# Remainders moved to VectorE, transposes of the probabilities and the projection moved within a pair, group means sooner

## The chip, the cores and the metric

The kernel runs on one core of one Trainium2 chip. The metric is the device time in microseconds (us) of one launch. Before the change it is 5577.6 us, the median of three runs (5576.49 to 5582.28).

## The reference

The input x is 8 images of 192 channels and 128x128 pixels. Two residual layers follow each other, each on a group norm of its input:

```python
# layer 1: attention in windows of 8x8 pixels, 6 heads of 32 channels
v, qk = x @ V_w.T + V_b, x @ QK_w.T + QK_b                # per pixel
o = irfft2(rfft2(q) * rfft2(k))                           # circular convolution in the window
attn = softmax(o @ v.T + bias)                            # 64x64 per head and window
y = attn @ v
x = x + (y @ proj_w.T + proj_b)
# layer 2: Laplacian and a 1x1 convolution
x = x + conv1x1(gn + laplacian(gn), merge_w) + merge_b    # gn = group_norm(x), 32 groups
```

The result has to be close to that of float32 throughout.

## The kernel before

**Units of work.** Two windows side by side are 128 pixels. The main loop works on doubles of such units: a *pair* in this text is one turn of `doubles()`, index j, 512 of them for the eight images, and four pairs make a *strip* of 8 image rows. The loop is a software pipeline written out by hand. In turn j the engines do step 0 of pair j (QKV, transposes of v), step 1 of pair j-1 (product in the frequency domain, inverse transform, scores), step 2 of pair j-2 (softmax), step 3 of pair j-3 (transposes of the probabilities, y) and step 4 of pair j-4 (projection). In the code `pair(k)` is true when there is a pair for step k.

**Engines.** Each engine runs its own list in the written order, and waits on semaphores (`wait_ge`). TensorE (PE) does the matmuls, ScalarE (ACT) copies from PSUM to SBUF and does the exponentials, VectorE (DVE) adds the position bias (L909, which writes `probs`), takes the maximum (L914), makes the remainders of q and k (L903), the frequency product (L920), the sum (L935), its reciprocal (L953), and the residual (L943). GpSimd (POOL) subtracts the maximum (L1225), multiplies by the reciprocal (L1246, semaphore `norm_done`), and computes the Laplacian of layer 2 (L1161, L1171, L1174) and the remainder of x (L1234). SyncE (SP) issues the DMAs.

**Two halves of a number.** float32 values are split into a rounded high part and a remainder, and matmuls of the parts are added. For the projection ACT writes the high parts `yh` and half of `yb` (`yh_out`), and POOL writes the remainders `yl` (L1251) and the other half of `yb` (L1253), each 256 columns, semaphore `yl_done`. `project()` (L582 to L587) does two matmuls on `yh`, then waits for `yl_done`, then does three more; it is called twice a pair, for channels 0 to 127 and 64 to 191.

**Banks.** `b_t` holds four PSUM banks. The frequency product L920 (`prod_done`) reads all four, and the transposes of the probabilities (L629) write two of them. QKV of the second unit writes `b_q` again, so it waits for the first unit's remainders (`lo_out`).

**Layer 2** runs 18 to 19 strips behind (`STENCIL_LAG`, `MERGE_LAG`), as "pieces" (L524 to L537) in the slots `m_slot` of the same loop: in a strip the pairs have two, one, two and one of them. The first 19 strips, 76 pairs, have none. POOL's Laplacian units come in three of the four pairs, and POOL's L1234 and DVE's `xhl` (L957) in every other one. DVE also reads the next image's statistics (L723), at the end of each pair in the first 12 of the 16 strips of the images 0 to 6. In the last 16 strips, after pair 512, only layer 2 is left, and VectorE shares the Laplacian with POOL (L854 to L859).

**Before the loop** the position bias is built in 64 steps of four matmuls (L493), with the group mean (L467), the group spread (L473) and the bias row (L480) of image 0 put between them.

## Time and profile before

| | us |
|---|---|
| median of three runs | 5577.6 |
| profiled execution, its own time | 5581.64 |
| its span | 5579.7 |
| PE busy | 5356.6 (96%) |
| DVE busy | 4229.7 (76%) |
| POOL busy | 4099.7 (73%) |
| ACT busy | 3757.7 (67%) |

The profiled execution ran at a mean granted TensorE clock of 0.995. Busy time of PE is modelled (matmuls overlap), so 96% means that PE nearly always has a matmul in flight; what it loses is seen in the time between the starts of successive matmuls. Times in the timelines are counted from the start of the span.

### The profile page before, as it was taken

What the parts mean: (1) busy time and instruction counts of PE and PEld (TensorE: products, weight loads), DVE (VectorE), ACT (ScalarE), POOL (GpSimd) and SP (SyncE); (2) the same over time, 40 slices, a digit from 0 to 9 for tenths busy, and PEclk for the clock granted to TensorE, in tenths of its full rate; (3) what the DMA queues carried; (4) which work ended last, traced back from release to release, by engine and by line L of the source; (5) the groups of instructions that cost most, each with busy time, mean ns of one, the idle gap of its engine ahead of it and who ended that gap; (6) DMA issues with size and microseconds to landing.
All of it is one profiled execution on the core that took longest, in us unless ns stands there. A gap on an engine that the chain in (4) does not pass through costs nothing.

```text
span 5579.7 us, 207720 instructions
## 1 busy us (share of the span) xinstructions
PE 5356.6 (96%) x90620; PEld 4638.2 (83%) x90620; DVE 4229.7 (76%) x6658; ACT 3757.7 (67%) x7653; POOL 4099.7 (73%) x3518
## 2 busy tenths in 40 slices
PE   7999999999999999999999999999999999999988
PEld 5888788888888888888888888888888888888865
DVE  5777677777777777787777877777777777777758
ACT  3666776667766677667676677666776677766643
POOL 1555557887887777878878777778778788787864
PEclk9999999999999999999999999999999999999989
DMA  4221123333333333432333333333333323233336
GB/s 139 63 74 55 51 74 106 113 93 94 109 111 108 88 105 103 115 107 84 104 113 108 104 85 107 114 106 99 93 107 111 113 85 88 81 85 86 87 98 181
DMA packets 392507, 550.39 MB, mean 99 GB/s; under 512 B 24822, under 2 KB 284729, under 8 KB 391610
## 3 DMA queue, kind: packets, MB, share of 16 engines
q1 hardware_dynamic: 391612, 537.11, 33.6%
q8 instruction: 726, 11.89, 0.9%
q14 instruction: 169, 1.38, 0.1%
HBM read 335.69 MB, written 201.33 MB: 96 GB/s over the span
## 4 chain that ended last, share of the span: by engine, by line
PE 67%; ACT 15%; POOL 12%; issue 3%; DVE 1%; DMA 1%; SPq 1%; POOLq 0%; ACTq 0%; DVEq 0%
PE b_q L576 18%; PE b_q L657 7%; PE b_t L671 6%; PE b_t L647 6%; PE b_s L689 5%; ACT probsT L970 3%; PE b_t L629 3%; ACT probs L1115 3%; PE b_s L524 3%; PE b_s L537 2%; PE b_s L526 2%; POOL yl L1251 2%; PE b_s L535 2%; POOL yb L1253 2%; PE b_s L585 2%
## 5 line engine op out<-in xcount | busy, mean ns | idle before, releaser
L1246 POOL TENSOR_TENSOR probs<-probs,srec 128x768 f32<-128x768 f32 x512 | 818.8, 1599 | 684.7 <-DVE srec L953 684.7
L909 DVE TENSOR_TENSOR probs<-b_s,posb 128x768 f32<-128x768 f32 x512 | 490.3, 958 | 675.9 <-PE b_s L689 673.9
L903 DVE TENSOR_TENSOR qkl<-b_q,qkh 128x384 fp32r<-128x384 f32 x1024 | 570.8, 557 | 514.7 <-ACT qkh L970 481.8
L970 ACT ACTIVATE vs<-b_q 128x192 f32<-128x192 f32 x1024 | 338.7, 331 | 784.1 <-PE b_q L576 784.1
L1225 POOL TENSOR_TENSOR probs<-probs,smax 128x768 f32<-128x768 f32 x512 | 755.0, 1475 | 57.2 <-DVE smax L914 17.8
L1251 POOL TENSOR_TENSOR yl<-yT,yh 128x256 fp32r<-128x256 f32 x512 | 376.0, 734 | 460.9 <-ACT yb L970 460.9
L576 PE MATMUL b_q<-wnh,xh 128*128 128x288 f32 x2048 | 670.4, 327 | 10.2 <-DVE qkl L903 7.1
L1161 POOL TENSOR_TENSOR dg<-late 128x645 f32<-128x645 f32 x352 | 563.0, 1599 | 68.1 <-DMA late<-x_dram 45.6
L970 ACT ACTIVATE qkh<-b_q 128x384 fp32r<-128x384 f32 x1024 | 497.7, 486 | 170.5 <-PE b_q L576 170.5
L576 PE MATMUL b_q<-wnl,xhl 128*128 128x288 f32 x2048 | 605.5, 296 | 0.0
L576 PE MATMUL b_q<-wnl,xh 128*128 128x288 f32 x2048 | 604.8, 295 | 0.0
L576 PE MATMUL b_q<-wnh,xhb 128*128 128x288 f32 x2048 | 603.1, 294 | 0.0
L576 PE MATMUL b_q<-wnh,xl 128*128 128x288 f32 x2048 | 602.6, 294 | 0.0
L970 ACT ACTIVATE yT<-b_t 128x512 f32<-128x512 f32 x512 | 305.8, 597 | 406.1 <-PE b_t L647 405.8
L689 PEld LDWEIGHTS b_s<-vT,osb 32*64 32x64 f32 x24576 | 412.4, 132 | 136.2 <-ACT osb L970 127.7
L943 DVE SCALAR_TENSOR_TENSOR late<-b_s,pb,xs 128x256 f32<-128x256 f32 (+1 forms) x1024 | 491.5, 480 | 16.9 <-PE b_s L587 9.4
L914 DVE TENSOR_REDUCE smax<-probs 128x12 f32<-128x768 f32 x512 | 488.2, 953 | 17.8
L689 PE MATMUL b_s<-vT,osb 32*64 32x64 f32 x24576 | 487.2, 222 | 3.8 <-issue 2.5
L935 DVE TENSOR_REDUCE ssum<-probs 128x12 f32<-128x768 f32 x512 | 482.6, 943 | 2.3 <-ACT probs L1115 2.3
L920 DVE TENSOR_TENSOR prod<-qh,b_t 128x768 f32<-128x768 f32 x512 | 483.6, 944 | 0.0
L1174 POOL TENSOR_TENSOR late<-late,dg 128x512 f32<-128x512 f32 x352 | 474.0, 1347 | 10.4
L657 PE MATMUL b_q<-inv_sb,prod 128*64 128x64 f32 x12288 | 472.1, 226 | 4.0 <-DVE qkl L903 3.3
(194 smaller groups left out, 15658.2 us busy)
## 6 DMA issues: line engine op xcount, KB each, us to landing
ld<-in_x SPq DMA_DIRECT2D x192, 512.0 KB, 4.6
late<-x_dram SPq DMA_DIRECT2D x112, 640.0 KB, 5.0
xs<-in_x SPq DMA_DIRECT2D x128, 512.0 KB, 4.0
x_dram<-late SPq DMA_DIRECT2D x128, 512.0 KB, 2.7
out<-late SPq DMA_DIRECT2D x128, 512.0 KB, 2.8
late<-x_dram SPq DMA_DIRECT2D x240, 192.0 KB, 5.5
xs<-in_x SPq DMA_DIRECT2D x128, 256.0 KB, 4.5
x_dram<-late SPq DMA_DIRECT2D x128, 256.0 KB, 3.5
```

What stands on the lines that cost most here:

```text
L576: last = mm(o, xx[:, h % 2, at], ww[:, par, t, lo:up], start=(k == 0), stop=(k == 4))
L657: last = mm(o_out_ps[g * N:(g + 1) * N, k * N:(k + 1) * N], prod[:, g * 6 + k, :, :].rearrange("p h d -> p (h d)"), inv[:, :], start=True, ...
L689: last = mm(scores[h * N:(h + 1) * N, s * N:(s + 1) * N], osb[r:r + HD, k, :], vT[r:r + HD, i % 2, part, q % 2 * N:q % 2 * N + N], start=T ...
L903: V.tensor_tensor(qkl[:, i % 2, :], q_out, qkh[:, i % 2, :].bitcast(F32), ALU.subtract).then_inc(lo_out, 1)
L909: V.tensor_tensor(scored(i).rearrange("p (t q) m -> p t q m", q=4), scores.rearrange("p (t q m) -> p t q m", q=4, m=N), posb[:, :, :].unsq ...
L914: V.tensor_reduce(smax[:, i % 2, :], scored(i), AX.X, ALU.max).then_inc(max_done, 1)
L943: last = V.scalar_tensor_tensor(out=x1s[0:m, t, u % 2, :].rearrange("p (r c) -> p r c", c=W)[:, :, col:col + 32], in0=src.rearrange("p (r ...
L970: return A.activation(o, i, ACT.Copy)
L1161: P.tensor_tensor(d, src[:, r + 1:r + 6, 0:W + 1], src[:, r:r + 5, 1:W + 2], ALU.add).then_inc(diag_done, 1)
L1225: P.tensor_tensor(probs[:, i % 2, :, :], probs[:, i % 2, :, :], smax[:, i % 2, :].unsqueeze(2).broadcast_to([128, 12, N]), ALU.subtract).t ...
L1246: P.tensor_tensor(probs[:, i % 2, :, :], probs[:, i % 2, :, :], srec[:, i % 2, :].unsqueeze(2).broadcast_to([128, 12, N]), ALU.mult).then_ ...
L1251: P.tensor_tensor(yl[:, :, :, :], y_a, yh[:, :, :, :].bitcast(F32), ALU.subtract).then_inc(yl_done, 1)
```

## The change

PE: the six transposes of the probabilities move from behind the transposes of v to ahead of the second QKV, and wait there for `norm_done` and `prod_done`; the first half of the projection moves from ahead of the second QKV to behind the transposes of v, next to the second half. In the first steps of the program, the group mean of image 0 is put at step 38 instead of 56, the spread at 41 instead of 58, the bias row at 57 and 61. DVE: the product comes ahead of the remainders, the maximum behind them; the remainders `yl` and `yb` are made here, in step 4, behind the maximum. ACT: the copy of the transposed probabilities comes ahead of the second copy of v, the exponentials, `weights` and `border` later. POOL: `yl` and `yb` go. SP: once the pairs are through, `source_load` is issued ahead of `result_store`.

```diff
@@ sync
                 double_started(4 * blk + 2)
+                v = blk - STENCIL_LAG + 1
+                if 4 * blk >= DOUBLES and 0 <= v < STRIPS:
+                    source_load(v)
                 v = blk - MERGE_LAG - 1
                 if 0 <= v < STRIPS:
                     result_store(v)
...
-                if 0 <= v < STRIPS:
+                if 4 * blk < DOUBLES and 0 <= v < STRIPS:
                     source_load(v)
@@ tensor, before the loop
-                if m == 56:
+                if m == 38:
                     group_mean(0)
-                elif m == 58:
+                elif m == 41:
                     group_spread(0)
-                elif m == 60:
+                elif m == 57:
                     bias(0, 0)
...
+                if m == 61:
+                    pe.wait_ge(m_read, 3)
+                    bias(0, 1)
...
-            pe.wait_ge(m_read, 3)
-            bias(0, 1)
@@ tensor, in the loop, behind m_slot(2 * j, pair)
-                if pair(4):
-                    n = pair(4)[1]
-                    pe.wait_ge(yh_out, n)
-                    if pair(2):
-                        pe.wait_ge(s_out, pair(2)[1])
...
-                    project(b_r[:, 0:256], 0, n)
+                if pair(3):
+                    k, n = pair(3)
+                    pe.wait_ge(norm_done, n)
+                    if pair(1):
+                        pe.wait_ge(prod_done, pair(1)[1])
+                    for i in range(2):
+                        for t in range(3):
+                            last = nc.tensor.transpose(
...
+                    last.then_inc(pT_mm, 1)
@@ tensor, behind the transposes of v (the transposes above stood here)
                 if pair(4):
-                    project(b_r[:, 256:512], CB, pair(4)[1]).then_inc(proj_mm, 1)
+                    n = pair(4)[1]
+                    pe.wait_ge(yh_out, n)
...
+                    project(b_r[:, 0:256], 0, n)
+                    project(b_r[:, 256:512], CB, n).then_inc(proj_mm, 1)
@@ vector
-                    dve.wait_ge(s_out, n)
-                    V.tensor_reduce(smax[:, i % 2, :], scored(i), AX.X, ALU.max).then_inc(max_done, 1)
-                if pair(0):
-                    remainders(2 * j)
                 if pair(1):
...
+                if pair(0):
+                    remainders(2 * j)
+                if pair(2):
+                    i, n = pair(2)
+                    dve.wait_ge(s_out, n)
+                    V.tensor_reduce(smax[:, i % 2, :], scored(i), AX.X, ALU.max).then_inc(max_done, 1)
+                if pair(4):
+                    dve.wait_ge(yh_out, pair(4)[1])
+                    V.tensor_tensor(yl[:, :, :, :], y_a, yh[:, :, :, :].bitcast(F32), ALU.subtract).then_inc(yl_done, 1)
+                    V.tensor_tensor(yb[CB:128, :, :, :], y_b[0:CB], yb[0:CB, :, :, :].bitcast(F32),
+                                    ALU.subtract).then_inc(yl_done, 1)
                 statistics(2 * j)
@@ scalar, behind split(h, 0 or 2)
+                if pair(3):
+                    act.wait_ge(pT_mm, pair(3)[1])
+                    copy(probsT[:, :, :, :].rearrange("p i h n -> p i (h n)"), q_banks[:, 0:2, 0:6 * N]
+                         ).then_inc(pT_out, 1)
                 if pair(0):
                     v_copy(2 * j + 1)
+                if pair(0):
+                    high(2 * j + 1)
...
                 if pair(2):
                     i, n = pair(2)
                     act.wait_ge(sub_done, n)
...
+                weights(blk, ph)
@@ gpsimd
-                if pair(3):
-                    pool.wait_ge(yh_out, pair(3)[1])
-                    P.tensor_tensor(yl[:, :, :, :], y_a, yh[:, :, :, :].bitcast(F32), ALU.subtract).then_inc(yl_done, 1)
-                    pool.wait_ge(yl_done, 2 * pair(3)[1] - 1)
-                    P.tensor_tensor(yb[CB:128, :, :, :], y_b[0:CB], yb[0:CB, :, :, :].bitcast(F32),
-                                    ALU.subtract).then_inc(yl_done, 1)
-                    pool.wait_ge(yl_done, 2 * pair(3)[1])
```

TensorE's list in a pair of the middle of the program, from the first piece to the second QKV (`probs` is the normalised softmax, `yh`, `yb`, `yl` the parts of y). Before:

```order
L524 MATMUL b_s<-late,mn 128x256
L526 MATMUL b_s<-late,mn 128x256
L582 MATMUL b_s<-yh,wph 128x256
L583 MATMUL b_s<-yh,wpl 128x256
L585 MATMUL b_s<-yb,wpl 128x256
L586 MATMUL b_s<-yb,wph 128x256
L587 MATMUL b_s<-yl,wph 128x256
L576 MATMUL b_q<-wnh,xh 128x288
```

and after (lines are 4 higher for the same function up to L591: L580 is QKV, L613 the transposes of the probabilities):

```order
L528 MATMUL b_s<-late,mn 128x256
L530 MATMUL b_s<-late,mn 128x256
L613 MATMUL b_t<-ident_sb,probs 128x128 x6
L580 MATMUL b_q<-wnh,xh 128x288
L580 MATMUL b_q<-wnl,xh 128x288
```

The five matmuls of the projection have gone from here, and the six transposes stand in their place.

The same list further on, from the transposes of v to the second piece. Before:

```order
L619 MATMUL b_t<-ident_sb,vs 128x128 x2
L620 MATMUL b_t<-ident_sb,vs 128x128
L621 MATMUL b_t<-ident_sb,vs 64x128
L629 MATMUL b_t<-ident_sb,probs 128x128 x6
L582 MATMUL b_s<-yh,wph 128x256
L583 MATMUL b_s<-yh,wpl 128x256
L585 MATMUL b_s<-yb,wpl 128x256
L586 MATMUL b_s<-yb,wph 128x256
L587 MATMUL b_s<-yl,wph 128x256
L524 MATMUL b_s<-late,mn 128x256
L526 MATMUL b_s<-late,mn 128x256
L647 MATMUL b_t<-probsT,vs 32x64 x24
```

and after:

```order
L628 MATMUL b_t<-ident_sb,vs 128x128
L629 MATMUL b_t<-ident_sb,vs 64x128
L586 MATMUL b_s<-yh,wph 128x256
L587 MATMUL b_s<-yh,wpl 128x256
L589 MATMUL b_s<-yb,wpl 128x256
L590 MATMUL b_s<-yb,wph 128x256
L591 MATMUL b_s<-yl,wph 128x256
L586 MATMUL b_s<-yh,wph 128x256
L587 MATMUL b_s<-yh,wpl 128x256
L589 MATMUL b_s<-yb,wpl 128x256
L590 MATMUL b_s<-yb,wph 128x256
L591 MATMUL b_s<-yl,wph 128x256
```

The transposes have gone, and all ten matmuls of the projection stand together, ahead of the second piece and of y.

VectorE's list from the start of a pair, with its waits. Before:

```order
L909 TENSOR_TENSOR probs<-b_s,posb 128x768 [waits s_mm]
L914 TENSOR_REDUCE smax<-probs 128x12 [waits s_out]
L903 TENSOR_TENSOR qkl<-b_q,qkh 128x384 [waits hi_out]
L920 TENSOR_TENSOR prod<-qh,b_t 128x4x3x64 [waits qh_out]
L828 BN_STATS bn<-late 64x6
L820 SCALAR_TENSOR_TENSOR late<-b_s,mc,late 128x256 [waits m_mm]
L903 TENSOR_TENSOR qkl<-b_q,qkh 128x384 [waits hi_out]
L935 TENSOR_REDUCE ssum<-probs 128x12 [waits exp_done]
```

and after (L912 was L909, L919 was L920, L906 was L903, L928 was L914; L931 and L932 are new):

```order
L912 TENSOR_TENSOR probs<-b_s,posb 128x768 [waits s_mm]
L919 TENSOR_TENSOR prod<-qh,b_t 128x4x3x64 [waits qh_out]
L906 TENSOR_TENSOR qkl<-b_q,qkh 128x384 [waits hi_out]
L928 TENSOR_REDUCE smax<-probs 128x12 [waits s_out]
L931 TENSOR_TENSOR yl<-yT,yh 128x256 [waits yh_out]
L932 TENSOR_TENSOR yb<-yT,yb 64x256
L831 BN_STATS bn<-late 64x6
L823 SCALAR_TENSOR_TENSOR late<-b_s,mc,late 128x256 [waits m_mm]
L906 TENSOR_TENSOR qkl<-b_q,qkh 128x384 [waits hi_out]
```

The maximum, for which POOL's subtraction waits, is now fourth, and between L931 and L932 there is no wait.

SyncE's list where the pairs end, from the last store of layer 1's result (L380). Before:

```order
L380 DMA x_dram<-late 128x1024
L381 DMA x_dram<-late 64x1024
L404 DMA out<-late 128x1024
L404 DMA out<-late 64x512 x2
L394 DMA late<-x_dram 128x9x128
L394 DMA late<-x_dram 64x5x128
L394 DMA late<-x_dram 64x6x128
```

and after:

```order
L380 DMA x_dram<-late 128x1024
L381 DMA x_dram<-late 64x1024
L394 DMA late<-x_dram 128x9x128
L394 DMA late<-x_dram 64x5x128
L394 DMA late<-x_dram 64x6x128
L404 DMA out<-late 128x1024
L404 DMA out<-late 64x512 x2
```

The loads of a strip now stand ahead of the stores of the same turn.

## Rows read from the trace of the kernel before

**Rows 1.** Waits over the whole span: who waited for whom: us, times, longest.

```profile
PEld b_t L647 <- ACT probsT L970: 144.0, 263, 1.9
```

**Rows 2.** Windows: one early pair, then four successive pairs: length, busy us of PE, PEld, DVE, ACT, POOL.

```profile
335.05:344.77 9.72, 8.90 (x174) 7.88 (x168) 7.75 (x12) 6.45 (x15) 6.09 (x5) 1.00 0.28 83
2995.64:3006.05 10.41, 10.33 (x183) 9.23 (x177) 8.02 (x14) 7.38 (x17) 5.26 (x5) 1.00 0.42 129
3006.05:3015.77 9.72, 9.41 (x179) 8.57 (x173) 8.13 (x13) 6.86 (x16) 8.74 (x8) 1.00 0.29 83
3015.77:3026.58 10.81, 10.75 (x185) 9.06 (x179) 7.82 (x13) 7.37 (x17) 9.43 (x8) 1.00 0.38 123
3026.58:3036.59 10.01, 9.69 (x180) 8.36 (x174) 8.68 (x13) 6.45 (x15) 9.03 (x8) 1.00 0.46 108
```

**Rows 3.** Timeline of PE, pair from 3006.05: start, length, engine, line.

```profile
3008.15 0.47 PE L582 MATMUL b_s<-yh,wph 128*128 128x256 f32 x1
...
3010.79 0.82 PE L629 MATMUL b_t<-ident_sb,probs 128*128 128x128 f32 x6
...
3011.80 0.28 PE L586 MATMUL b_s<-yb,wph 128*128 128x256 f32 x1
...
3011.92 0.28 PE L587 MATMUL b_s<-yl,wph 128*128 128x256 f32 x1
...
3012.51 0.73 PE L647 MATMUL b_t<-probsT,vs 64*32 64x64 f32 x48 [0.31 <-ACT probsT L970]
...
3014.91 0.93 PE L689 MATMUL b_s<-vT,osb 32*64 32x64 f32 x48
```

**Rows 4.** Timeline of DVE (VectorE), the same pair.

```profile
3006.18 0.96 DVE L909 TENSOR_TENSOR probs<-b_s,posb 128x768 f32<-128x768 f32 x1 [1.52 <-PE b_s L689]
...
3007.17 0.95 DVE L914 TENSOR_REDUCE smax<-probs 128x12 f32<-128x768 f32 x1
...
3008.20 0.56 DVE L903 TENSOR_TENSOR qkl<-b_q,qkh 128x384 fp32r<-128x384 f32 x1
...
3008.67 0.94 DVE L920 TENSOR_TENSOR prod<-qh,b_t 128x768 f32<-128x768 f32 x1
...
3010.14 0.47 DVE L820 SCALAR_TENSOR_TENSOR late<-b_s,mc,late 128x256 f32<-128x256 f32 x1
...
3011.32 0.56 DVE L903 TENSOR_TENSOR qkl<-b_q,qkh 128x384 fp32r<-128x384 f32 x1 [0.72 <-ACT qkh L970]
...
3013.80 0.69 DVE L957 TENSOR_TENSOR xhl<-xs,xhl 64x512 fp32r<-64x512 f32 x1
...
3014.52 0.69 DVE L723 BATCH_NORM_STATS2 bn<-ld 128x6 f32<-128x512 f32 x1
```

**Rows 5.** Timeline of POOL (GpSimd), the same pair.

```profile
3008.41 1.48 POOL L1225 TENSOR_TENSOR probs<-probs,smax 128x768 f32<-128x768 f32 x1
...
3012.64 1.28 POOL L1234 TENSOR_TENSOR xl<-xs,xh 128x512 fp32r<-128x512 f32 x1
...
3013.88 1.65 POOL L1174 TENSOR_TENSOR late<-late,dg 128x512 f32<-128x512 f32 x1
...
3015.50 1.47 POOL L1246 TENSOR_TENSOR probs<-probs,srec 128x768 f32<-128x768 f32 x1
```

**Rows 6.** Source view of L752, start of the program: duration ns min/median/max, first and last start.

```profile
L752 DVE TENSOR_SCALAR wn<-wq,cst x2: 521/1018/1515, 72.8 to 73.2; 128x576 f32<-128x576 f32 x2
```

**Rows 7.** Timeline of POOL at the same moment.

```profile
72.86 1.54 POOL L1234 TENSOR_TENSOR xl<-xs,xh 128x512 fp32r<-128x512 f32 x1 [71.75 <-ACT xh L970]
```

**Rows 8.** Timelines of POOL and DVE in the last strips.

```profile
5437.86 2.20 POOL L1161 TENSOR_TENSOR dg<-late 128x645 f32<-128x645 f32 x1 [5.20 <-ACT late L1026]
...
5438.69 1.92 DVE L857 TENSOR_TENSOR late<-late,probs 128x512 f32<-128x512 f32 x1
```

**Rows 9.** Chain of waits in the first 110 us: start, length, what.

```profile
44.41 24.06 PE b_q L493 x448
```

**Rows 10.** Source view of L854: idle of VectorE before it and what ended it.

```profile
  issue: 5.1, 8
```

More of the change, by code:

```diff
@@ L601, in _ @@
                 m_slot(2 * j, pair)
-                if pair(4):
-                    n = pair(4)[1]
-                    pe.wait_ge(yh_out, n)
-                    if pair(2):
-                        pe.wait_ge(s_out, pair(2)[1])
-                    elif pair(5):
-                        pe.wait_ge(x1_done, pair(5)[1])
-                    project(b_r[:, 0:256], 0, n)
+                if pair(3):
[6 more added lines that the diff above has]
+                            last = nc.tensor.transpose(
+                                q_banks[:, i, t * 128:(t + 1) * 128],
+                                probs[:, k % 2, 4 * t + 2 * i:4 * t + 2 * i + 2, :].rearrange("p w m -> p (w m)"),
+                                ident[:, :])
+                    last.then_inc(pT_mm, 1)
                 if pair(0):
@@ L621, in _ @@
                     nc.tensor.transpose(vt_out[0:CB, 2, :], vs[:, at, CA:C], ident[:, :]).then_inc(vT_mm, 1)
-                if pair(3):
-                    k, n = pair(3)
-                    pe.wait_ge(norm_done, n)
-                    if pair(1) and not pair(0):
-                        pe.wait_ge(prod_done, pair(1)[1])
-                    for i in range(2):
-                        for t in range(3):
-                            last = nc.tensor.transpose(
-                                q_banks[:, i, t * 128:(t + 1) * 128],
-                                probs[:, k % 2, 4 * t + 2 * i:4 * t + 2 * i + 2, :].rearrange("p w m -> p (w m)"),
-                                ident[:, :])
-                    last.then_inc(pT_mm, 1)
-                if pair(4):
-                    project(b_r[:, 256:512], CB, pair(4)[1]).then_inc(proj_mm, 1)
+                if pair(4):
+                    n = pair(4)[1]
+                    pe.wait_ge(yh_out, n)
+                    if pair(2):
+                        pe.wait_ge(s_out, pair(2)[1])
+                    elif pair(5):
+                        pe.wait_ge(x1_done, pair(5)[1])
+                    project(b_r[:, 0:256], 0, n)
+                    project(b_r[:, 256:512], CB, n).then_inc(proj_mm, 1)
                 m_slot(2 * j + 1, pair)
@@ L923, in _ @@
                                     ALU.mult).then_inc(prod_done, 1)
+                if pair(0):
+                    remainders(2 * j)
+                if pair(2):
+                    i, n = pair(2)
[6 more added lines that the diff above has]
+                                    ALU.subtract).then_inc(yl_done, 1)
                 statistics(2 * j)
@@ L1105, in _ @@
                 split(h, 0 if j % 2 == 0 else 2)
-                weights(blk, ph)
-                if ph == 0 and 0 <= blk - STENCIL_LAG < STRIPS:
-                    border(blk - STENCIL_LAG)
+                if pair(3):
+                    act.wait_ge(pT_mm, pair(3)[1])
+                    copy(probsT[:, :, :, :].rearrange("p i h n -> p i (h n)"), q_banks[:, 0:2, 0:6 * N]
+                         ).then_inc(pT_out, 1)
                 if pair(0):
                     v_copy(2 * j + 1)
+                if pair(0):
+                    high(2 * j + 1)
+                    act.wait_ge(vT_mm, pair(0)[1])
+                    copy(vT[:, j % 2, :, :], vt_out).then_inc(vT_out, 1)
                 if pair(2):
@@ L1115, in _ @@
                     A.activation(pr, pr, ACT.Exp).then_inc(exp_done, 1)
-                if pair(0):
-                    high(2 * j + 1)
-                    act.wait_ge(vT_mm, pair(0)[1])
-                    copy(vT[:, j % 2, :, :], vt_out).then_inc(vT_out, 1)
-                if pair(3):
-                    act.wait_ge(pT_mm, pair(3)[1])
-                    copy(probsT[:, :, :, :].rearrange("p i h n -> p i (h n)"), q_banks[:, 0:2, 0:6 * N]
-                         ).then_inc(pT_out, 1)
+                weights(blk, ph)
+                if ph == 0 and 0 <= blk - STENCIL_LAG < STRIPS:
+                    border(blk - STENCIL_LAG)
                 a_result(2 * j + 1)
```

1 line of the change is left out of this document (removed).

## The prediction

> **What bounds the kernel now.** I read four views: windows of single pairs, the waits, the timelines of one pair, and places where VectorE and GpSimd (POOL) meet. Four successive pairs take 10.41, 9.72, 10.81 and 10.01 us, together 40.95; an early pair, without layer 2, takes 9.72 [rows 2]. TensorE is busy for 9.4 of 9.72, and its list is tight: in the pair that starts at 3006.05, which I count as 0, the first piece ends and the projection starts at 2.10, the transposes of the probabilities at 4.74, the last projection matmul at 5.87, y at 6.46, the scores at 8.86 [rows 3]. One hole is left: successive projection matmuls start 0.12 apart, y comes 0.59 after the last, with 0.31 idle put down to ScalarE's copy `probsT` [rows 3]; over the span the weight loads of y lose 144 us in 263 waits to it [rows 1]. VectorE is busy for 8.1 of 9.72 and POOL for 8.7 [rows 2], so neither is the bound, but both hand work to TensorE. In the same count, VectorE does L909 at 0.13, the maximum from 1.12 to 2.07, L903 at 2.15, the product from 2.62 to 3.56, the second L903 at 5.27, `xhl` at 7.75, the statistics from 8.47 to 9.16 [rows 4]. POOL subtracts the maximum at 2.36 and ends its last step, the normalising L1246, at 3016.97, 10.92, which is 1.20 into the next pair [rows 5]. That was harmless: the transposes wanted it at 4.74.
>
> **The port.** Where VectorE reads two SBUF operands, it and POOL exclude each other. In the last strips VectorE's L857 takes 1.92 us when POOL's L1161 runs; L957, also of 512 columns, takes 0.69 [rows 8, 4]. At the start of the program two L752 stand back to back with no wait between. The first took 0.52, the second, from 73.2, 1.52: POOL's L1234 had asked at 72.86 and got in between, until 74.40 [rows 6, 7]. An operation that waits seems to begin 0.14 before the recorded end of the other (L857 ends at 5440.61, 0.69 earlier is 5439.92; L1161's recorded end is 5440.06) [rows 8]. `yl` and `yb` read yT and yh or yb, all in SBUF, so I let them behave like these. The Trainium skill ("SBUF — State Buffer", "Who interferes with whom") has the same in general: a VectorE instruction with two SBUF inputs and a GpSimd instruction that reads SBUF hold an exclusive lock, and the second one blocks fully. No row here has `yl` on VectorE; by that rule it is as I assume, and without it the sum would be the third case below.
>
> **The change in the short pair (9.72).** VectorE: L909 0.13 to 1.09; the product follows at once, to about 1.96; L903 again at 2.15, since it waits for ScalarE, to 2.71; the maximum about 2.63 to 3.58. POOL can subtract from 3.66 at the earliest; before it was 2.36. `yl` starts at 3.50. Its price: L909 has 768 columns for 0.96, L903 384 for 0.56, so 256 cost about 0.42; bounds are half of `xhl`'s 0.69 and L820's 0.47, which reads 256 columns [rows 4]. `yb` ends by twice the difference sooner or later: -0.14 or +0.10 a pair, -70 or +50 us over 512 pairs. `yl` ends at 3.92 and lets POOL in at 3.78, so the subtraction (1.48) [rows 5] ends at about 5.25; `yb`, which stands next with no wait, is shut out until 5.11 and ends at 5.53. This is the core: two operations of 0.42 take 2.0 us. TensorE: QKV and piece to 2.10 as before, then the transposes (product 1.96, normalising: below), which take about what the half projection took there, so the transposes of v end near 4.74 and two matmuls on `yh` near 5.0. The third waits for `yb`: 5.53 plus 0.15 = 5.68 (the 0.15 is my reading of an answer from VectorE to TensorE). Eight matmuls remain, 0.12 apart with 0.1 allowed for the restart: the last starts at 6.60. ScalarE's copy of the probabilities has long been done, so y comes 0.2 behind, at 6.80; the hole of 0.39 is closed, but y is 0.34 later than its 6.46. From y to the next pair is 3.26 [rows 2, 3]: the pair takes 10.06, 0.34 more. Where the piece is longer (the pair of 10.01) the wait hides behind it: also 10.06.
>
> **The next pair.** VectorE: the result piece and statistics like L820 and L723, then L903 again at 6.44; from L903 to `xhl` is 2.48 [rows 4], so `xhl` is due at 8.92. POOL: from 5.25 `yb` holds it to 5.39, then the two Laplacian steps, L1234 to about 9.46. `xhl` waits for that, ends at 10.01; L1174 and L1246 follow, L1246 ends at about 12.48 (its way from subtraction to end was 8.56, is 8.7 from 3.78) [rows 5]. That is 2.42 into the next pair, and the transposes want it now at 2.10, not at 4.74. VectorE's statistics end at 10.7, so L909 of the next pair is at 0.60 instead of 0.13, the product ends at 2.42, and the transposes start at 2.57. The maximum ends at 3.77, `yb` at 5.72, the third projection matmul is at 5.87, the last at 6.79. Behind it, by the shape of these pairs, come the second piece and y at 7.86 or 8.21, and the pair takes 11.12 (was 10.41) or 11.47 (was 10.81). ScalarE's exponentials and VectorE's sums end in time for the scores (9.2 against 8.9), so the later `exp`, `weights` and `border` cost nothing; their cover is TensorE's work up to the scores, and beyond its 0.3 each 0.1 would move the scores by 0.1.
>
> **The sum.** A strip: 10.06 + 11.47 + 10.06 + 11.12 = 42.71 against 40.95, +1.76. Without statistics L723 VectorE is on time at 0.14, and the two long pairs gain 0.19 each: +1.38. 109 of 128 strips carry layer 2; 69 of them have L723, 40 not: 69 x 1.76 + 40 x 1.38 = 177. The 76 early pairs cost 0.34 each: 26. The front: 448 matmul records of L493 are 56 steps in 24.06, 0.43 each [rows 9]; the mean is put 18 steps sooner, 7.7 us, and the chain behind it to the first QKV starts that much sooner, with TensorE's own list needing nearly all of the time: -7 (bounds 0 and -7.7). The tail: VectorE waited 5.1 us before its first stencil operation in 8 strips for no partner that the trace names [rows 10]; loads issued sooner may return part: -3 (bounds 0 and -5). Together 177 + 26 - 7 - 3 = +193 on the profiled execution's own 5581.6 (span 5579.7); it stands 4 above the median. Forecast 5577.6 + 193 = about 5770.
>
> **Rivals.** *VectorE keeps the port* from `yl` through `yb`, since nothing separates them. Then `yb` ends at 4.26, the projection never waits, the odd pairs take 9.35 and 9.61. But POOL's subtraction starts at 4.12, L1246 ends at 12.65, 3.30 into the next pair, and `xhl` shifts VectorE so that the product ends there at 3.29. The long pairs wait 1.3 and 1.1: 11.83 and 11.20. Strip 41.99, +1.04; 109 x 1.04 = 113, early pairs -0.37 each = -28, ends -10: 5653. Rows 6 and 7 speak against.
> *No exclusion for these two*, so that only `xhl` meets POOL: short pairs 9.27 and 9.62, POOL's chain ends 2.9 into the next, long pairs 11.4 and 10.75: strip 41.04, +0.1; with -30 and -10, 5550. It is faster by 0.5%; rows 8 speak against it.
> *The transposes never wait*: the same, and L1246 always done at 2.10, as if POOL lost nothing by the later maximum. Strip 9.27 + 10.47 + 9.62 + 10.17 = 39.5, -1.4: -153 - 30 - 10 gives 5385. For it: the hole of rows 1. Against: POOL starts 1.3 later and was 1.20 into the next pair already [rows 5], 2.5 against 2.10.
> *Nothing moves*: the transposes' wait takes just what the hole gives: 5575.
> *Worse*: POOL wins the port ahead of `yl` too, then both come behind the subtraction, `yb` at 5.95 or behind the next operation: at least 0.42 x 512 = 215 more, 5985.
>
> **Chances.** Forecast 0.70 (own range 5700 to 5840), VectorE keeps the port 0.09, no exclusion 0.08, never waits 0.05, nothing moves 0.05, worse 0.03. That is faster by over 0.2% (about what a measurement of this kernel can tell from no change) 0.13, within 0.05, slower 0.82. The range 5640 to 5850 takes in the forecast's bounds and the kept port; it leaves out no exclusion, never waits, nothing moves and worse, together 0.21.
>
> **What would show it.** Right: `yb` (now L932) takes about 1.7 us with `yl` at 0.42; TensorE waits at L589 for VectorE's `yb` in nearly every pair; POOL's subtraction starts 3.7 to 3.8 into the pair; L613 waits in every second pair, for `norm_done` or the product; `probsT` leaves the waits of y; pairs of 10.1, 11.5, 10.1, 11.1. The first QKV starts at about 84 instead of 91. Wrong: `yb` at 0.42 (second case), POOL's operations untouched (third), or L613 without a wait (fourth).

## The result, and the profile after

The changed kernel takes 5816.3 us (median of four runs, 5807.33 to 5819.72) against 5577.1 (5573.07 to 5582.28): a ratio of 1.0429, 95% interval 1.0416 to 1.0442. It is slower by 239 us, where +193 was forecast. Its profiled execution took 5807.33 us, the lowest of the four, with a span of 5805.5 and a mean granted clock of 0.996 (0.995 before); the other three executions had 0.993 and 0.994.

The page: busy times of the engines; the chain that ended last; then groups of instructions, with busy time and mean ns of one, and behind the second bar the idle time ahead of them.

```profile
PE 5501.8 (95%) x90620; PEld 4631.8 (80%) x90620; DVE 5128.6 (88%) x7682; ACT 3842.7 (66%) x7653; POOL 3484.1 (60%) x2494
...
PE 49%; DVE 44%; ACT 4%; issue 3%; POOL 1%; SPq 0%; DMA 0%; POOLq 0%; DVEq 0%; ACTq 0%
...
L1235 POOL TENSOR_TENSOR probs<-probs,smax 128x768 f32<-128x768 f32 x512 | 812.1, 1586 | 1489.8 <-DVE smax L928 1489.8
L932 DVE TENSOR_TENSOR yb<-yT,yb 64x256 fp32r<-64x256 f32 x512 | 808.9, 1580 | 15.8
```

VectorE went from 76% to 88% busy, and 44% of the chain runs over it, where it was 1% before. Its busy time rose by 899 us, and one new operation has 809: `yb`, 1.58 us each, of 256 columns. Its twin `yl` of the same columns takes 0.42 in the timeline below. POOL lost two operations, and waits 1490 us for the maximum.

Five windows, one early pair and four successive ones, answer to [rows 2]: stretch in us, its length, and busy time (with the count of instructions) by engine.

```profile
core 0: us, PE busy (x) PEld busy (x) DVE busy (x) ACT busy (x) POOL busy (x), PEclk, DMA share, GB/s
328.10:338.07 9.97, 9.03 (x175) 7.84 (x169) 9.50 (x14) 6.70 (x15) 4.50 (x4) 1.00 0.28 82
3131.48:3141.65 10.17, 9.65 (x179) 8.55 (x173) 9.70 (x15) 7.22 (x16) 6.44 (x5) 1.00 0.27 79
3141.65:3153.02 11.37, 11.02 (x179) 8.99 (x179) 10.12 (x16) 7.31 (x16) 9.45 (x7) 1.00 0.37 118
3153.02:3163.17 10.15, 10.01 (x181) 8.40 (x175) 9.68 (x15) 6.78 (x15) 6.43 (x5) 1.00 0.47 105
3163.17:3174.34 11.17, 10.82 (x176) 9.20 (x176) 10.13 (x16) 7.32 (x16) 5.39 (x4) 1.00 0.38 119
```

Together 42.86 where 42.71 was forecast and 40.95 stood before; singly 10.17, 11.37, 10.15, 11.17 for a forecast of 10.06, 11.47, 10.06, 11.12. PEclk, the granted clock, is 1.00 in all of them, so the clock has no part in these pairs. It has one at two other places, which come below.

The short pair that starts at 3131.48, first on VectorE (start, duration, line, operation, and in brackets the idle time ahead and what ended it), answers to [rows 4]:

```profile
3134.11 0.94 DVE L928 TENSOR_REDUCE smax<-probs 128x12 f32<-128x768 f32 x1
3134.97 0.42 DVE L931 TENSOR_TENSOR yl<-yT,yh 128x256 fp32r<-128x256 f32 x1
3135.41 1.58 DVE L932 TENSOR_TENSOR yb<-yT,yb 64x256 fp32r<-64x256 f32 x1
...
3140.49 1.02 DVE L967 TENSOR_TENSOR xhl<-xs,xhl 64x512 fp32r<-64x512 f32 x1
3141.53 0.69 DVE L726 BATCH_NORM_STATS2 bn<-ld 128x6 f32<-128x512 f32 x1
```

On POOL, to [rows 5]:

```profile
3135.13 1.59 POOL L1235 TENSOR_TENSOR probs<-probs,smax 128x768 f32<-128x768 f32 x1 [4.10 <-DVE smax L928]
3136.68 1.76 POOL L1171 TENSOR_TENSOR dg<-late 128x645 f32<-128x645 f32 x1
...
3139.66 1.30 POOL L1244 TENSOR_TENSOR xl<-xs,xh 128x512 fp32r<-128x512 f32 x1
```

And on TensorE, to [rows 3]:

```profile
3133.77 0.82 PE L613 MATMUL b_t<-ident_sb,probs 128*128 128x128 f32 x6
...
3136.39 0.28 PE L587 MATMUL b_s<-yh,wpl 128*128 128x256 f32 x1
3137.05 0.38 PE L589 MATMUL b_s<-yb,wpl 128*128 128x256 f32 x1 [0.38 <-DVE yb L932]
...
3138.18 0.72 PE L650 MATMUL b_t<-probsT,vs 64*32 64x64 f32 x48
```

Read them together. `yl` runs alone. POOL's subtraction starts at 3.65 of the pair and its record ends at 5.24; `yb` stands on VectorE from 3.93 and is recorded until 5.51, so the two "run" side by side, but `yb` does its 0.4 us of work only at the end. TensorE's third projection matmul starts at 5.57, 0.66 behind the second. The copy `probsT` no longer stands ahead of y: it comes 0.2 behind the last projection matmul, at 6.70 instead of 6.46. `xhl` is shut out until 10.03 in the same way. That has two effects. First, the next QKV needs `xhl`. It starts at 10.17, 0.14 behind the recorded end of `xhl` and 1.07 behind the start of the scores, where 0.86 is usual; without that wait the pair would have taken 6.70 + 3.26 = 9.96, as the early pairs do. Over the pairs with layer 2, QKV of the even pair starts 0.15 behind `xhl` in the median; before the change it was 1.27. Second, VectorE's L912 of the next pair moves to 0.61, and a piece of layer 2 on TensorE waits for it:

```profile
3143.36 0.67 PE L528 MATMUL b_s<-late,mn 128*128 128x256 f32 x2
3143.87 0.59 PE L530 MATMUL b_s<-late,mn 128*128 128x256 f32 x2
```

The piece starts at 1.71 of that pair, against 1.43 in the short one, and the transposes (L613) at 2.65. The waits over the span:

```profile
PEld b_s L589 <- DVE yb L932: 226.0, 505, 2.0
PE b_s L589 <- DVE yb L932: 113.9, 336, 1.8
...
PE b_t L613 <- DVE prod L919: 37.8, 73, 0.9
...
PE b_s L528 <- DVE probs L912: 24.3, 102, 1.3
...
PEld b_t L613 <- POOL probs L1256: 23.7, 57, 2.3
```

PEld is the loading of weights and PE the matmuls; both lines at L589 tell of the same waits, so they don't add up. Like for like, the weight loads lose 226.0 us at L589 in place of the 144.0 of [rows 1]. The 73 waits of L613 for the product are in the early pairs, which have no piece ahead of it.

### The profile page after: what moved, and what is told of

Its sections match the earlier page's. It is cut to its first block, busy times and chain, and to the rows that moved or that the text cites. A ratio compares the mean times of both kernels' runs of the same rounds, so it can differ in the third digit from the quotient of the medians.

```text
span 5805.5 us, 207717 instructions
## 1 busy us (share of the span) xinstructions
PE 5501.8 (95%) x90620; PEld 4631.8 (80%) x90620; DVE 5128.6 (88%) x7682; ACT 3842.7 (66%) x7653; POOL 3484.1 (60%) x2494
## 4 chain that ended last, share of the span: by engine, by line
PE 49%; DVE 44%; ACT 4%; issue 3%; POOL 1%; SPq 0%; DMA 0%; POOLq 0%; DVEq 0%; ACTq 0%
DVE yb L932 12%; PE b_q L580 11%; DVE smax L928 7%; PE b_t L674 6%; PE b_s L692 6%; PE b_q L660 5%; DVE qkl L906 5%; PE b_t L650 4%; ACT qkh L980 3%; PE b_s L589 3%; DVE yl L931 3%; DVE xhl L967 2%; DVE late L953 2%; DVE ssum L945 2%; DVE probs L912 2%
## 5 line engine op out<-in xcount | busy, mean ns | idle before, releaser
L1235 POOL TENSOR_TENSOR probs<-probs,smax 128x768 f32<-128x768 f32 x512 | 812.1, 1586 | 1489.8 <-DVE smax L928 1489.8
L1256 POOL TENSOR_TENSOR probs<-probs,srec 128x768 f32<-128x768 f32 x512 | 777.6, 1519 | 610.9 <-DVE srec L963 610.9
L912 DVE TENSOR_TENSOR probs<-b_s,posb 128x768 f32<-128x768 f32 x512 | 490.3, 958 | 421.2 <-PE b_s L692 411.7
L932 DVE TENSOR_TENSOR yb<-yT,yb 64x256 fp32r<-64x256 f32 x512 | 808.9, 1580 | 15.8
L580 PE MATMUL b_q<-wnh,xh 128*128 128x288 f32 x2048 | 696.8, 340 | 30.7 <-DVE xhl L967 9.4
L980 ACT ACTIVATE probsT<-b_t 128x768 f32<-128x768 f32 x512 | 416.8, 814 | 362.1 <-PE b_t L613 362.1
L1171 POOL TENSOR_TENSOR dg<-late 128x645 f32<-128x645 f32 x352 | 619.5, 1760 | 57.9 <-DMA late<-x_dram 35.8
L906 DVE TENSOR_TENSOR qkl<-b_q,qkh 128x384 fp32r<-128x384 f32 x1024 | 562.1, 549 | 96.2 <-ACT qkh L980 95.6
L580 PE MATMUL b_q<-wnl,xhl 128*128 128x288 f32 x2048 | 606.1, 296 | 0.0
L580 PE MATMUL b_q<-wnl,xh 128*128 128x288 f32 x2048 | 604.4, 295 | 0.0
L580 PE MATMUL b_q<-wnh,xhb 128*128 128x288 f32 x2048 | 602.5, 294 | 0.0
L580 PE MATMUL b_q<-wnh,xl 128*128 128x288 f32 x2048 | 602.2, 294 | 0.0
L1184 POOL TENSOR_TENSOR late<-late,dg 128x512 f32<-128x512 f32 x352 | 513.8, 1460 | 10.4
L919 DVE TENSOR_TENSOR prod<-qh,b_t 128x768 f32<-128x768 f32 x512 | 483.4, 944 | 1.4 <-ACT qh L980 1.4
L928 DVE TENSOR_REDUCE smax<-probs 128x12 f32<-128x768 f32 x512 | 482.5, 942 | 0.0
```

The lines of the kernel that those rows point to most:

```text
L580: last = mm(o, xx[:, h % 2, at], ww[:, par, t, lo:up], start=(k == 0), stop=(k == 4))
L906: V.tensor_tensor(qkl[:, i % 2, :], q_out, qkh[:, i % 2, :].bitcast(F32), ALU.subtract).then_inc(lo_out, 1)
L912: V.tensor_tensor(scored(i).rearrange("p (t q) m -> p t q m", q=4), scores.rearrange("p (t q m) -> p t q m", q=4, m=N), posb[:, :, :].unsq ...
L928: V.tensor_reduce(smax[:, i % 2, :], scored(i), AX.X, ALU.max).then_inc(max_done, 1)
L932: V.tensor_tensor(yb[CB:128, :, :, :], y_b[0:CB], yb[0:CB, :, :, :].bitcast(F32), ALU.subtract).then_inc(yl_done, 1)
L980: return A.activation(o, i, ACT.Copy)
```

## The experiments

Each kernel was timed against the kernel before on its own chip (5575.7 to 5580.1, median). Ratios are to it, with 95% intervals.

**One operand instead of two.** In the changed kernel (indices and signals not shown; the kernel leaves out the subtraction, so y's projection has other values):

```diff
-  V.tensor_tensor(yl, y_a, yh, ALU.subtract)
-  V.tensor_tensor(yb[CB:128], y_b[0:CB], yb[0:CB], ALU.subtract)
+  V.tensor_reduce(yl, y_a.unsqueeze(4), AX.X, ALU.max)
+  V.tensor_reduce(yb[CB:128], y_b[0:CB].unsqueeze(4), AX.X, ALU.max)
```

> The changed kernel, but yl and yb are made by a maximum over an axis of length one, which reads one SBUF operand (yT) instead of two; same columns, same place, same signals. The low parts are then not remainders, so y's projection has other values. Theory 1 (VectorE and POOL exclude each other, where VectorE reads two SBUF operands): both operations take about 0.42 us, POOL's subtraction 1.47 from 3.66 into the pair, TensorE's wait for yb disappears; what stays is that the transposes of every second pair wait for POOL's normalising. Short pairs about 9.3, long ones 10.8 and 11.3; 5530 to 5590 us. Rival (VectorE is simply too full: 0.84 us more work in each pair, busy 88%): same work, so the time stays at 5816 within 20 us.

Measured: 5575.3, ratio 0.9992 [0.9982, 1.0001]. VectorE and POOL at the same place, in the pair that starts at 3042.47:

```profile
3045.95 0.41 DVE L932 TENSOR_REDUCE yl<-yT 128x256 fp32r<-128x256 f32 x1
3046.40 0.41 DVE L933 TENSOR_REDUCE yb<-yT 64x256 fp32r<-64x256 f32 x1
3046.84 0.70 DVE L831 BATCH_NORM_STATS2 bn<-late 128x6 f32<-128x512 f32 x1
```

```profile
3046.12 1.48 POOL L1235 TENSOR_TENSOR probs<-probs,smax 128x768 f32<-128x768 f32 x1 [4.07 <-DVE smax L928]
```

Same place, same columns, same neighbour on POOL, one SBUF operand fewer: 0.41 instead of 1.58, and some 241 us of the time. The exclusion is shown; VectorE's load (two operations more) costs nothing that can be measured.

**`yl` and `yb` back on POOL**, at the end of its list as before; every other edit of the change kept.

```diff
@@ vector
-                if pair(4):
-                    ... yl and yb as in the change
@@ gpsimd, behind the normalising
+                if pair(3):
+                    ... yl and yb as in the kernel before
```

> The changed kernel with one part undone: yl and yb are made by POOL again, at the end of its list as before; the orders of TensorE, VectorE and ScalarE and the two ends stay changed. Theory 1: POOL makes them while it waits for the maximum, so they cost nothing there; the hole before y is closed; what remains is that POOL's normalising and VectorE's xhl end late in the short pairs, and the transposes of the long pairs wait 0.6 to 0.9 us: short pairs 9.3 and 9.65, long ones 11.3 and 10.8, strip 41.1; 5530 to 5580 us. Rival (the early transposes are the whole loss): stays above 5750.

Measured: 5580.8, ratio 1.0003 [0.9994, 1.0013]; 0.8 above the expected range and 26 above its middle; the other edits together are worth nothing that can be measured. The first step is right: in the short pair y starts at 6.05 to 6.1 instead of 6.46, and the scores end at 9.40. But the next pair's QKV starts only at 9.92. The waits put 54.5 us to `xhl`, in 145 pairs. POOL begins its chain at 3.7 instead of 2.36, and so it is in its Laplacian and `xl` when `xhl` comes (8.26 to 9.78, recorded).

**`yb` behind the statistics and the result piece**, `yl` left in its place.

```diff
                     V.tensor_tensor(yl, ...)
-                    V.tensor_tensor(yb[CB:128], ...)
                 statistics(2 * j)
                 m_result(2 * j)
+                if pair(4):
+                    V.tensor_tensor(yb[CB:128], ...)
```

> The changed kernel, but on VectorE the statistics and the result piece stand between yl and yb, so that they run while POOL holds the port. Theory 1: yb still ends at about 5.5, since it can start only when POOL's subtraction is over, and the short pairs stay at 10.15; but VectorE is through 1.1 us sooner, so the long pairs lose their late start: 11.05 and 10.9 instead of 11.37 and 11.17; strip 42.3, 5740 to 5770 us. Rival (only the wait of TensorE for yb counts): no change against 5816, within 15 us.

Measured: 5789.1, ratio 1.0374 [1.0358, 1.0389]; outside what was expected, above the range of the theory and below that of the rival. `yb` now takes 0.60 (median), from 4.92 to 5.51 of the pair, and VectorE's second remainders come 1 us sooner; but `yb` ends no earlier, TensorE waits at L589 as before, and `xhl` is still recorded until 10.00, with the next QKV at 10.15. So the long pairs do not gain as was thought: two in a row took 11.03 and 11.37, where 10.9 and 11.05 were expected. And pair 5 of the images 2 to 7 takes 12.9 (11.3 in the changed kernel), with the granted clock below 1 in it. An order on VectorE that fills the blocked time gives back 27 of 239 us.

**POOL's order.** As the kernel with `yl` and `yb` on POOL; POOL's `xl` ahead of the subtraction, where POOL is idle, and VectorE's last statistics ahead of `xhl`.

> e1 (y's remainders on POOL, early transposes) with two more moves: POOL makes the remainder of x (xl) while it waits for the maximum, ahead of the subtraction, and VectorE does the statistics ahead of xhl. Theory 1: POOL's normalising of the short pairs ends 1.3 us sooner, at 1.7 into the next pair, VectorE starts the next pair 0.7 sooner; the transposes wait 0.1 to 0.3: short pairs 9.3 and 9.65, long ones 10.7 and 10.35, strip 40.0 against 40.9 before; 5420 to 5470 us, faster than both kernels. Rival (TensorE's transposes ahead of QKV cannot pay): not under 5577.

Measured: 5579.9, ratio 1.0000 [0.9990, 1.0009]: missed by over 100 us. The transposes no longer wait for POOL (their weight loads lose 2.7 us in one wait, against 23.7 in 57 in the changed kernel), and the short pair still ends late. TensorE behind the scores of the pair that starts at 3054.43:

```profile
3062.89 0.93 PE L692 MATMUL b_s<-vT,osb 32*64 32x64 f32 x48
3064.30 0.37 PE L580 MATMUL b_q<-wnh,xh 128*128 128x288 f32 x1 [0.49 <-DVE xhl L965]
```

VectorE beside it:

```profile
3063.24 0.92 DVE L965 TENSOR_TENSOR xhl<-xs,xhl 64x512 fp32r<-64x512 f32 x1
```

QKV of every even pair waits for `xhl`. It is made in the last microsecond of the odd pair. In the kernel before it was late once (2.7 us); here the matmuls of QKV lose 113.4 us to it in 173 waits. Both expectations left out this wait: a hole was closed ahead of another wait, which then took its time.

**`xhl` sooner.** Two kernels, each with one edit on VectorE. The first is the one with POOL's order, the second the one with only `yl` and `yb` back on POOL.

```diff
                 if pair(0):
                     remainders(2 * j + 1)
+                if j % 2 == 0 and 0 <= h < PAIRS // 4:
+                    dve.wait_ge(xh_done, 3 * h + 1)
+                    V.tensor_tensor(tokens(xhl, 1, h, CB), ...).then_inc(xhl_done, 1)
...
-                if j % 2 == 1 and 0 <= h < PAIRS // 4:
-                    ... xhl
```

> As v1_pool_order, and VectorE makes xhl in the even pair ahead, behind the second remainders of q and k, where VectorE was idle for 0.7 us; both high parts that it reads are there by then. Theory (the short pairs of v1 and e1 end late because QKV of the next pair waits for xhl, which GpSimd's Laplacian holds up): QKV follows the scores at once, the short pairs take 9.35 and 9.7 instead of 9.87 and 10.4, the even pairs stay at 10.15 and 10.5; a strip is 39.7 against 41.16 in v1, the early pairs gain too: 5380 to 5440. Rival (the odd pairs end late for another reason, ScalarE's yb or POOL's L1251, which would push the next pair): QKV still starts at 9.9 and the time stays at 5560 to 5580.

> As e1_y_on_pool (yl and yb on GpSimd, its own order untouched), and only xhl moved as in v2. Odd pairs 9.35 and 9.7. GpSimd ends its normalising about 2.5 into the even pair, since it lacks v1's order, so the transposes wait 0.4 there as in e1: even pairs 10.65 and 10.9, a strip 40.6 against 41.28 in e1: 5460 to 5520. If xhl were not what holds the odd pairs, 5580 as e1.

Measured: 5512.4, ratio 0.9877 [0.9864, 0.9891], and 5542.5, ratio 0.9933 [0.9920, 0.9947]. The mechanism holds: in the pairs looked at, QKV follows the scores at once, short pairs take 9.31 and 9.75, and `xhl` as the end of QKV's wait is left once. The sizes fall short, by 72 and 22 us. Part of it stands on VectorE in the pair that starts at 3012.41, the one with two outputs of layer 2:

```profile
3017.99 1.68 DVE L940 TENSOR_TENSOR xhl<-xs,xhl 64x512 fp32r<-64x512 f32 x1
...
3021.72 0.48 DVE L823 SCALAR_TENSOR_TENSOR late<-b_s,mc,late 128x256 f32<-128x256 f32 x1
```

and on POOL:

```profile
3017.56 1.58 POOL L1166 TENSOR_TENSOR dg<-late 128x645 f32<-128x645 f32 x1
3019.21 1.51 POOL L1176 TENSOR_TENSOR late<-late,dg 128x512 f32<-128x512 f32 x1
```

`xhl` stands behind `dg`, gets in between it and L1176 (1.51 instead of 1.19), and ends 1 us late; the result piece L823 comes at 9.31 instead of 8.23, the scores wait for the bank that it reads, and the pair takes 10.92 instead of 10.52.

**ScalarE's order.** The changed kernel with ScalarE's `weights` and `border` put back ahead of the second copy of v.

> The changed kernel with one edit undone: ScalarE's weights and border stand again ahead of the second copy of v and the exponentials (here also ahead of the copy of the probabilities). Theory: the 3.4 us that pair 11 of each image loses against before (14.8 instead of 11.4) come from the scaled merge matrices, which ScalarE writes behind its exponentials and two table loads, so that TensorE's mean matmuls start at 9.0 instead of 6.6. Then that pair takes about 12.2 and the time falls by 8 times 2.6 to 4: 5784 to 5797. Rival: that pair is held by VectorE (as pairs 4 and 5 of an image are), and the time stays at 5816.

Measured: 5807.6, ratio 1.0407 [1.0391, 1.0423]; 9 below the changed kernel, half of the least expected, and the two intervals overlap. The profiles agree on the size: up to the start of the last pair this kernel needs 8.8 us less. Pair 11 of an image in the changed kernel, ScalarE, then TensorE:

```profile
3639.46 1.28 ACT L1130 ACT_TABLE_LOAD   x1
3640.76 0.84 ACT L1130 ACTIVATE probs<-probs 128x768 f32<-128x768 f32 x1
3641.51 0.49 ACT L1074 ACTIVATE mn<-wm,sm 128x256 f32<-128x256 f32 x1
3641.90 0.60 ACT L1075 ACTIVATE mn<-wm,sm 128x384 f32<-128x384 f32 x1
```

```profile
3640.11 0.28 PE L591 MATMUL b_s<-yl,wph 128*128 128x256 f32 x1
3642.65 0.35 PE L515 MATMUL b_s<-sm,mn 128*128 128x1 f32 x2 [2.26 <-ACT mn L1075]
```

With the edit undone that wait is gone and the pair takes 11.3 instead of 14.8, less than the 12.2 of the theory. The loss was not the wait alone. Behind it TensorE's granted clock fell to the lower of its two levels (1.2 GHz) for part of the pair: 0.89 on average in this pair, and it fell in pair 11 of each of the images 1 to 7; with the edit undone it fell in none. What the clock costs by itself is seen in the kernel with `xhl` in the even pair, where the same wait stands in every pair 11 but the clock does not always fall:

```profile
2778.74:2791.98 13.24, 10.70 (x189) 9.29 (x183) 7.50 (x13) 8.51 (x16) 10.55 (x14) 1.00 0.36 82
3434.80:3449.51 14.71, 12.15 (x189) 10.51 (x183) 7.50 (x13) 8.98 (x17) 10.55 (x14) 0.88 0.33 72
```

That is 1.2 to 1.5 us (the other pair 11 at full clock took 13.54). The kernel before has pair 11 at 11.0 in six of these images and at 13.7 in one, where the clock fell as well; from 11.0 to 14.7, the wait of 2.26 and the clock are the whole loss. Against the gain, pair 10 is 1.0 longer with the edit undone, and so is pair 52 (12.0 instead of 11.0), where, as I read it, other steps of `weights` now stand ahead of v and the exponentials. In the fast schedule below the same edit is worth 22 us: pair 11 gives back 28.5 over the seven images there, and pair 10 costs 8.3.

**The place of `xhl`, again**, with and without ScalarE's edit: `xhl` behind the first remainders of the even pair.

> As v2_xhl_even, with two edits: VectorE makes xhl behind the first remainders of q and k of the even pair, when GpSimd is done with yb (2.3) and waits for the maximum (3.7), so that nobody is shut out; and ScalarE's weights and border stand ahead of the second copy of v, as in e8. Theory (in v2 the pair with two outputs of layer 2 takes 10.92 instead of 10.5 because xhl waits there for GpSimd's Laplacian from 5.6 to 7.3, and with it the result piece L823 that the scores wait for): that pair takes 10.5, a strip 39.9 against 40.31, and pair 11 of an image 11.3 instead of 14.2: 5430 to 5480. Rival: the maximum that comes 0.7 later in the even pairs costs as much through the exponentials and the sum as is won, 5490 to 5510.

> As v5_xhl_first without the edit on ScalarE, to part the two gains. Expected 8 to 25 us above v5, as e8 stood 8 below the changed kernel: 5445 to 5500. If the place of xhl is worth nothing, 5512 as v2.

Measured: 5499.3, ratio 0.9863 [0.9848, 0.9878], and 5521.6, ratio 0.9902 [0.9888, 0.9917]. Both miss their range, the first by 19 us, into that of its rival, the second by 22. `xhl` takes 0.69 there, and the pair of 10.92 takes 10.55, as expected; but the other even pair, 10.18, takes 10.55 too, since L823 ends at 9.43 in it as well. Without ScalarE's edit this is no better than the kernel with `xhl` behind the second remainders: a strip of pairs 12 to 43 is 40.28 against 40.31, a gain of 0.37 in one pair and the same loss in another.

**Each place where it is good.**

```diff
-                if j % 2 == 0 and ...:     # xhl behind the first remainders
+                if j % 4 == 2 and ...:
+                if j % 4 == 0 and ...:     # and this behind the second
```

> As v5_xhl_first, but xhl has its place by pair: behind the first remainders where GpSimd's Laplacian runs later in the pair (every fourth pair), behind the second remainders where GpSimd is idle there (the even pairs between). v5's profile shows that the later maximum makes the even pairs 10.55 where v2 had 10.18, since the result piece L823 ends at 9.43 and the scores wait for it; v2's shows 10.92 where v5 has 10.55. If both theories hold the two gains add: pairs of 10.18, 9.31, 10.55 and 9.75 to 10.0, a strip of 39.9 against 40.26: 5455 to 5475. If not, 5500 as v5.

Measured: 5470.0 (5466.61 to 5473.24), ratio 0.9807 [0.9791, 0.9823], within what was expected. Both theories hold. The four pairs:

```profile
2977.98:2988.14 10.16, 10.16 (x182) 9.06 (x176) 8.51 (x14) 7.50 (x17) 5.42 (x5) 1.00 0.42 131
2988.14:2997.45 9.31, 9.31 (x179) 8.45 (x172) 7.29 (x12) 7.01 (x16) 8.23 (x8) 1.00 0.30 88
2997.45:3008.00 10.55, 10.55 (x185) 8.97 (x179) 8.50 (x14) 7.66 (x17) 8.60 (x8) 1.00 0.39 127
3008.00:3017.75 9.75, 9.75 (x180) 8.40 (x175) 7.29 (x12) 6.67 (x15) 9.44 (x9) 1.00 0.49 110
```

39.77 together, and the profile shows no idle TensorE in them. This version beats both kernels: 109 us less than before, and some 346 less than the changed one.

**Only the two ends** of the change, in the kernel before: the means sooner, and `source_load` ahead of `result_store`.

> The kernel before with only the two edits outside the pairs: the group mean, spread and bias row put sooner in the 64 steps ahead of the loop, and, once the pairs are through, source_load issued ahead of result_store. If what the trace of the changed kernel shows at its two ends comes from these edits alone, the first scored pair starts 7 us sooner, the stretch behind the last pair is some 10 to 19 us shorter, nothing else moves, and the time is 17 to 26 us below before: 5552 to 5562. Rival: the tail's gain came from the order in the pairs (VectorE and POOL end their last work otherwise), then only the front remains, about 5571.

Measured: 5564.5, ratio 0.9972 [0.9961, 0.9982]; the gain is real, 16 us, 2.5 short of the expected range. Between the profiles, 4.0 come from the front (first scored pair at 104.0 instead of 108.0) and 11.1 from the stretch behind the last pair, mostly in the steps of the last strips.

**Only `yl` and `yb` moved**, in the kernel before: behind the maximum on VectorE, all orders as they were.

> The kernel before with only one part of the change: yl and yb on VectorE, behind the maximum; the first half of the projection still stands ahead of the second QKV. Theory: yl from 2.0 to 2.5, GpSimd's subtraction from 2.2 to 3.7 shuts yb out, which ends near 4.1; the third projection matmul starts at 4.25 instead of 2.53, the first remainders come at 4.1 to 4.7, and the second QKV, which waits for both, starts at 4.8 instead of 2.89: 1.9 more a pair, less 0.3 from the hole before y: 6400 to 6600. Rival (without exclusion): yb ends at 2.9, the pair loses 0.5 to 0.8, about 5850 to 6000.

Measured: 6530.7, ratio 1.1713 [1.1694, 1.1733], within what was expected. VectorE and TensorE in the pair that starts at 3603.64:

```profile
3605.64 0.41 DVE L917 TENSOR_TENSOR yl<-yT,yh 128x256 fp32r<-128x256 f32 x1
3606.08 1.58 DVE L918 TENSOR_TENSOR yb<-yT,yb 64x256 fp32r<-64x256 f32 x1
```

```profile
3607.72 0.38 PE L585 MATMUL b_s<-yb,wpl 128*128 128x256 f32 x1 [1.39 <-DVE yb L918]
...
3608.40 0.37 PE L576 MATMUL b_q<-wnh,xh 128*128 128x288 f32 x1
```

The third projection matmul is at 4.08 and the second QKV at 4.76 of the pair, 4.25 and 4.8 expected. Not all of the 955 us are this wait at full clock: up to 1045 us the mean granted clock is 0.91 (1.00 from there to the last pair). Of the pairs 4 to 47 those in which it falls take 13.1, the others 11.6; for the 52 pairs in which it falls that makes about 75 us, an estimate. The expectation had left that out. The other edits of the change together hide some 700 us of what this move costs alone; as I read it, that is the projection's later place, but no run has that edit by itself.

## Why the prediction was right, and where its sizes were off

**The port.** The step that carries the forecast, `yb` shut out while `yl` is not, came as written: 1.58 against 0.42, ended at 5.51 (5.53 forecast), L589 at 5.57 (5.68), y at 6.70 (6.80). It is shown twice: with one operand less it vanishes, and moved alone into the kernel before it comes again at another time of the pair. The rival in which VectorE keeps the port through both is out by these rows, and so is the one without exclusion. What that rival would have given, the first experiment shows: 5575 and not 5550. Its strip is 0.24 longer than before, not 0.1 (`xhl`, for which QKV waits 38.7 us), and pair 11 costs 24 us that the rival's sum lacks. By the Trainium skill's rule ("SBUF — State Buffer", "Who interferes with whom") the second to ask is blocked, and the rows agree.

**A strip.** Forecast +1.76, measured +1.86 in the strips of an image's pairs 12 to 43 (40.92 to 42.79). The chain over `xhl` to the late L912 is as forecast (0.61 for 0.60). What follows from it was not as forecast in two places, and there the close sum is in part luck. *The long pairs*: the forecast had the transposes wait in every second pair, for the product or for POOL, from 2.57. TensorE waits one step earlier, at the piece L528, which cannot start before L912 is done (24.3 us in 102 waits), and that happens to put the transposes at 2.65; L613 waits for POOL 57 times in the span. *The short pairs*: the forecast has `xhl` end at 10.01 and, by its own 0.15 for an answer from VectorE, should have had the next QKV at 10.16, but it let QKV follow the scores at 10.06. Measured is 10.17. Without `xhl` it would be 9.96, since L589 came 0.1 sooner than forecast; an error of -0.1 and a wait of +0.2 that the forecast lacks partly cancel. The rows of three kernels agree on this wait: `xhl` ends at 9.78, 10.00 and 10.03, and QKV starts at 9.92, 10.15 and 10.17. No run moves `xhl` alone in the changed kernel.

**The sum of the spans,** +225.8 between the profiles (of the +239 between medians, 9 are that the profile after is the lowest of its runs, and 5 that the one before was above its median):

| | forecast | measured |
|---|---|---|
| front | -7 | -7.2 |
| early pairs | +26 | +14.3 |
| the other pairs | +177 | +238.2 |
| behind the last pair | -3 | -19.4 |

The sum is 33 us too low, and it would be 61 but for the 28 that the early pairs and the end give back; the forecast came close to the time by such errors against each other too. Three terms were mis-sized. *The other pairs*: 108.75 strips at 1.86 are 202. The remaining 36 fall on pairs near an image's boundary. "The later `exp`, `weights` and `border` cost nothing" was wrong for `weights`: pair 11 loses 3.4 us (11.4 to 14.8), 24 us over the seven images, of which the wait for the merge matrices is one part and the lower clock behind it the other. The experiment on ScalarE gives it back, though not without a cost in pairs 10 and 52. Pairs 4 and 5 lose 1.5 each, 18 us over six images: they have a second L831 of 0.69 behind `yb`, and the second remainders, at 7.13 instead of 6.54, are late for L660. The experiments on the port bear that reading out: with `yb` at 0.41, or on POOL, these two pairs together lose 0.4, not 3.0. And "without L723 +1.38" took VectorE to be on time there: the strip of pairs 60 to 63 loses 1.85. *The early pairs* take 9.95 to 9.97, not 10.06, since the wait is answered 0.06 behind `yb` and not 0.15. *Behind the last pair*: the forecast sized only the wait for loads; the two ends alone give 11 of the 19, in the strips' steps. The other 8 go with the clock of this one execution. From the start of the last pair the mean granted clock is 0.94 in it and the stretch takes 216.4; the kernel with ScalarE's edit has 0.89 and 224.6, the one with only the two ends 0.91 and 224.7, the one before 0.90 and 235.8. The changed kernel's other three executions had a lower mean clock and took 9 to 12 us longer, so its median seems to hold no such gain. Why the clock held there once stays open.

**Would the change gain without the port?** The rival "the transposes never wait" (5385) says so. In three runs the port is out of the way at `yb` and the hole of [rows 1] is closed, and the time is unchanged (0.9992, 1.0003, 1.0000); in a fourth `xhl` moves as well, and it falls by 1.2%. Unchanged is a sum here. With `yl` and `yb` on POOL the profile gains 6.8 us at the front, 17.8 in the early pairs and 13.4 behind the last pair, and loses 38.9 in the pairs between, 25 of them at pair 11. So the closed hole paid in the pairs without layer 2, and two other waits took the gain back: QKV's for `xhl`, and TensorE's for ScalarE's matrices, with the lower clock behind it.

## What to carry to other kernels

An operation of 0.4 us costs what its neighbour on the other engine lasts, if both want the same port: read its price from where it will stand, not from its size. A hole in a tight list is worth only the slack up to the next wait; before closing it, list every other wait of the same stretch with the time at which it is answered. A time that stays the same can be a gain and a loss at different places: compare stretch by stretch, and look at the granted clock behind every long wait of TensorE. When a move gains in one pair and loses in another, give each its own place.

## What the runs showed of the hardware

Two operations back to back on VectorE, both with two SBUF operands, are not one claim on the port: POOL, which asked during the first, got in between them in all 512 pairs (`yb`'s least time is 1.29). In the same way `xhl` got in between two of POOL's that stand 0.08 apart, and made the second last 1.51 instead of 1.19. The recorded duration of a blocked operation holds the wait, so busy shares overstate work: 88% of VectorE here, about 600 us of it waiting in `yb`. The reduction over an axis of length one, with one SBUF operand, copies at the subtraction's speed (0.41) and is not held up. A wait of TensorE of 2.3 us between matmuls can cost more than itself: behind it the granted clock fell in five to seven of the seven pairs 11 of every kernel that has the wait, and the pair took 1.2 to 1.5 us more than where it stayed at 1.00.
